# Attention probabilities turned by 32x32 blocks on VectorE and through DRAM instead of by TensorE transposes

## Chip, cores and metric

The kernel runs on one core of one Trainium2 chip. The metric is the device time of one execution in microseconds, as the median of several runs.

## What is computed

Two rows x of 1024 tokens by 512, float32. Cut to what matters:

```python
xn = layernorm(x)
q = rmsnorm(xn @ Wq.T, q_w)      # 32 heads of 128
k = rmsnorm(xn @ Wk.T, k_w)      # 8 kv heads of 128, 4 query heads on each
v = xn @ Wv.T
scores = q @ k.T / sqrt(128) + slope[head] * (j - i), masked to j <= i
s = softmax(scores) @ v          # heads side by side: 4096
s = s @ Wo.T                     # 4096 -> 512
g = silu(down(silu(xn @ w_gate.T) * (xn @ w_up.T)))   # inner size 1376
out = x + s * g
```

## The kernel before

Every matmul operand is held as two float32r parts, a high half (a ScalarE copy) and a low half (the value less its high half, made by VectorE or GpSimd), and every product is three matmuls: high x high, high x low, low x high.

For each of the 2 rows the kernel runs 8 units, one per kv group, and then the feed-forward part in chunks. A unit has 8 steps, one per query tile of 128 tokens. In step i, TensorE projects tile i+2 (`project`, lines 337 to 353), multiplies the attention tile of i-2 with w_o (`out_project`, 406), makes tile i's scores (`scores`, 366) in chunks of at most 512 keys per head, two score banks in turn, and between them turns and weighs tile i-1 block by block: `turn_probs` (381) turns the 128 keys of a block for the four heads by four TensorE transposes (line 388) into one of three ring banks, and `weigh` (392) multiplies the turned block with v (line 401). A unit has 36 such blocks. Then it turns q and k of tile i+1 (lines 359 and 364) in the same ring. The order is written out by hand in a `step` function for each engine, and each engine runs its own in order; semaphores count the results.

ScalarE squares the projections (line 569), stages v (574), copies the turned blocks' high halves out of the ring (`high_probs`, 597), takes exps in place with the row sum (`exp`, 589) and the high half of the attention tile (602). VectorE sums the squares (749), scales q and k (784), makes their low halves (790, 796), adds bias and mask and finds the row minimum (`bias`, 810, a main instruction and a read of the accumulator), divides the probabilities by their row sum (`divide`, 828), makes the blocks' low halves from the ring bank (`low_probs`, 818) and that of the attention tile (832), and adds to y (841). GpSimd has the chain of 13 small instructions for the norms (1016 to 1033), the low halves of w_qkv (1046), w_o (1052), v (1039, 1041) and of the feed-forward weights (1065, 1070). SyncE issues all transfers (`alone` is a wait, line 222). Probabilities lie in two buffers, one for even tiles and one for odd.

Of the kernel before, what the change touches and what calls it, by code (L numbers as in the profile page):

```python
# [47 lines left out]
CHUNK_WIDTH = [(i + 1) * P // HEAD_CHUNKS[i] for i in range(TILES)]  # L48
# [3 lines left out]
BEFORE = [TILES] + list(range(1, TILES))  # L52
RING_PER_STEP = 2
TURN_AT = [sum(BEFORE[1:i + 1]) - BEFORE[i] for i in range(TILES)] + [TURNS - TILES]
RBANKS = 3
RING = TURNS + RING_PER_STEP * TILES
RING_AT = [RING_PER_STEP - TILES]
for _i in range(TILES):
    RING_AT.append(RING_AT[-1] + BEFORE[_i] + RING_PER_STEP)
RING_AT[TILES] -= RING_PER_STEP  # L60

SKIPS = [RING_AT[2], RING_AT[5]]
RING_BANK = [(r + sum(r >= skip for skip in SKIPS)) % RBANKS for r in range(RING)]
assert (RING + len(SKIPS)) % RBANKS == 0
SLOTS = 4
LAG = 2

def ring_bank(r):

    return RING_BANK[r % RING]

def last_use(r):

    return next(q for q in range(r - 1, r - 2 * RBANKS, -1) if ring_bank(q) == ring_bank(r))

def turn_qk_at(i, turns, last):

    return turns - 1 if last and i >= TILES - 3 else turns + 1

def shape_of_step(i, first):

    chunks = G * HEAD_CHUNKS[i] if i < TILES else 0
    turns = 0 if first and i == 0 else TILES if i == TILES else BEFORE[i]
    return chunks, turns, max(chunks, turns + LAG if turns else 0)

def build(nc, x, w_qkv, w_o, w_ffn, q_norm, k_norm, rel, slopes, inv_slopes, ident_in, out):
    ctx = ExitStack()
    with ctx:
# [18 lines left out]
        probs = [sb("probs0", [P, G, S - P]), sb("probs1", [P, G, S])]  # L112
        pT_hi, pT_lo = sb("pT_hi", [P, SLOTS, G * P], F32R), sb("pT_lo", [P, SLOTS, G * P], F32R)
        attT_hi, attT_lo = sb("attT_hi", [P, G * P], F32R), sb("attT_lo", [P, G * P], F32R)
        natural = sb("natural", [P, 3 * NQK])
        qk = [natural[:, k * NQK:(k + 1) * NQK] for k in range(2)]
        qk_sq = natural[:, 2 * NQK:3 * NQK]
        v_nat = sb("v_nat", [P, VBUFS, P])
        rel_sb, ident = sb("rel_sb", [P, S]), sb("ident", [P, P])
# [3 lines left out]
        row_sum, rec = sb("row_sum", [P, 2, G]), sb("rec", [P, G])  # L123
        sq_sum, rq = sb("sq_sum", [P, G + 1]), sb("rq", [P, G + 1])
# [11 lines left out]
        probs0 = probs[0][:, :, :].rearrange("p g n -> p (g n)")  # L136
# [68 lines left out]
        def score_of(n, width, first):  # L205

            if first and n < G:
                return out_ps[:, 0:width] if n % 2 == 0 else ring_ps[:, ring_bank(1), 0:width]
            return score_ps[:, n % 2, 0:width]

        def early(t):

# [957 lines left out]
```

## Time and profile before

| | before |
|---|---|
| median of 3 runs | 2454.9 us (2453.91 to 2457.38) |
| the profiled execution's own time | 2455.46 us |
| its span | 2453.7 us, granted TensorE clock 0.998 |
| TensorE / VectorE / ScalarE / GpSimd busy | 99% / 69% / 50% / 31% |
| data moved | 92.19 MB, 38 GB/s on average |

The busy share is the time in which an engine had an instruction under way. The span runs from the first to the last instruction. A VectorE or ScalarE instruction may begin shortly before the one ahead has ended, so the sum of durations is somewhat above the busy time.

### The profile page before, as it was taken

Reading aid. Unit: us, or ns where it says so; the run is one execution under the profiler, and the core shown is the slowest. Engines: PE = TensorE matmul, PEld = TensorE weight load, DVE = VectorE, ACT = ScalarE, POOL = GpSimd, SP = SyncE. Lnnn points to the kernel's source line nnn. Section 1 sums busy time; section 2 is a strip of 40 time slices with the busy share of each in tenths; the row PEclk is TensorE's granted clock in tenths of the full one; section 3 lists DMA queues with packets and bytes.
Section 4 is the critical chain, followed back from the end, with each engine's and each line's share of the span. In section 5 each row is a group of like instructions: output and inputs, shape, how many; then the busy total and the mean of one; then the engine's idle time right before and its main releaser. Section 6 shows DMA issues by size and latency. Waiting matters only on the chain.

```text
span 2453.7 us, 37432 instructions
## 1 busy us (share of the span) xinstructions
PE 2422.6 (99%) x13232; PEld 2070.7 (84%) x13232; DVE 1693.7 (69%) x3788; ACT 1236.1 (50%) x2548; POOL 756.9 (31%) x2053
## 2 busy tenths in 40 slices
PE   7999999999999999999999999999999999999998
PEld 6888888888888888878888888888888888888887
DVE  7777777777778787823377787777777777777132
ACT  4555554555545555543355555555555545545333
POOL 2323231413233323244522232323232314131443
PEclk9999999999999999999999999999999999999999
DMA  3010000000000000023320101010000000010232
GB/s 130 1 40 4 27 18 27 18 27 18 27 18 27 18 27 18 27 91 125 112 78 1 44 1 44 1 44 1 27 18 26 18 27 18 1 44 14 90 103 103
DMA packets 23289, 92.19 MB, mean 38 GB/s; under 512 B 6592, under 2 KB 6720, under 8 KB 19136
## 3 DMA queue, kind: packets, MB, share of 16 engines
q1 hardware_dynamic: 23104, 89.80, 10.5%
q8 instruction: 106, 1.74, 0.3%
q14 instruction: 79, 0.65, 0.1%
HBM read 85.60 MB, written 4.19 MB: 37 GB/s over the span
## 4 chain that ended last, share of the span: by engine, by line
PE 96%; DVE 2%; ACT 1%; issue 1%; POOL 0%; DMA 0%; DVEq 0%; ACTq 0%; POOLq 0%
PE out_ps L401 17%; PE score_ps L377 16%; PE out_ps L414 14%; PE qkv_ps L351 14%; PE ring_ps L388 10%; PE qkv_ps L352 7%; PE score_ps L504 5%; PE qkv_ps L504 4%; PE ring_ps L520 4%; PE ring_ps L359 2%; PE out_ps L520 1%; PE ring_ps L364 1%; PE score_ps L351 0%; DVE y L997 0%; DVE xT_lo L868 0%
## 5 line engine op out<-in xcount | busy, mean ns | idle before, releaser
L597 ACT ACTIVATE pT_hi<-ring_ps 128x512 fp32r<-128x512 f32 x576 | 344.0, 599 | 509.8 <-PE ring_ps L388 497.2
L818 DVE TENSOR_TENSOR pT_lo<-ring_ps,pT_hi 128x512 fp32r<-128x512 f32 x576 | 396.8, 690 | 90.6 <-ACT pT_hi L597 86.0
L589 ACT ACTIVATE probs<-probs,low_min 128x896 f32<-128x896 f32 (+7 forms) x512 | 395.2, 774 | 50.4 <-DVE low_min L810 50.1
L1016 POOL TENSOR_SCALAR rs_x<-sq_sum 128x5 f32<-128x5 f32 x122 | 24.8, 203 | 1128.1 <-DVE sq_sum L749 1128.1
L388 PE MATMUL ring_ps<-ident,probs 128*128 128x128 f32 x2304 | 345.6, 273 | 0.0
L388 PEld LDWEIGHTS ring_ps<-ident,probs 128*128 128x128 f32 x2304 | 281.7, 140 | 42.1
L810 DVE CUSTOM_DVE_ANT_0 probs<-score_ps,rel_sb,slope 128x512 f32<-128x512 f32 (+5 forms) x504 | 301.7, 599 | 5.7 <-PE score_ps L377 4.3
L377 PE MATMUL score_ps<-kv_hi,qT_hi 128*128 128x320 f32 (+4 forms) x760 | 275.6, 363 | 3.0 <-DVE xT_lo L868 2.0
L401 PE MATMUL out_ps<-pT_hi,kv_hi 128*128 128x512 f32 x576 | 265.8, 461 | 2.9 <-DVE pT_lo L818 2.6
L377 PE MATMUL score_ps<-kv_hi,qT_lo 128*128 128x320 f32 (+4 forms) x760 | 261.0, 343 | 0.0
L377 PE MATMUL score_ps<-kv_lo,qT_hi 128*128 128x320 f32 (+4 forms) x760 | 260.3, 342 | 0.0
L828 DVE TENSOR_SCALAR probs<-probs,rec 128x896 f32<-128x896 f32 (+7 forms) x512 | 233.1, 520 | 4.5
L569 ACT ACTIVATE natural<-qkv_ps 128x640 f32<-128x640 f32 x124 | 87.7, 708 | 286.4 <-PE qkv_ps L352 286.4
L401 PE MATMUL out_ps<-pT_hi,kv_lo 128*128 128x512 f32 x576 | 227.5, 395 | 0.0
L401 PE MATMUL out_ps<-pT_lo,kv_hi 128*128 128x512 f32 x576 | 225.6, 392 | 0.0
L414 PE MATMUL out_ps<-o_hi,attT_hi 128*128 128x512 f32 x512 | 204.1, 399 | 0.0
L351 PE MATMUL qkv_ps<-qkv_hi,xT_hi 128*128 128x512 f32 x496 | 199.1, 401 | 1.8 <-DVE natural L784 1.8
L414 PE MATMUL out_ps<-o_hi,attT_lo 128*128 128x512 f32 x512 | 200.9, 392 | 0.0
L414 PE MATMUL out_ps<-o_lo,attT_hi 128*128 128x512 f32 x512 | 200.2, 391 | 0.0
L351 PE MATMUL qkv_ps<-qkv_hi,xT_lo 128*128 128x512 f32 x496 | 196.0, 395 | 0.0
L351 PE MATMUL qkv_ps<-qkv_lo,xT_hi 128*128 128x512 f32 x496 | 195.8, 395 | 0.0
L810 DVE CUSTOM_DVE_ANT_0 probs<-score_ps,rel_sb,low_min 128x320 f32<-128x320 f32 (+3 forms) x256 | 180.8, 706 | 21.0 <-PE score_ps L377 18.8
(178 smaller groups left out, 5293.5 us busy)
## 6 DMA issues: line engine op xcount, KB each, us to landing
qkv_raw<-w_ffn_dram SPq DMA_DIRECT2D x44, 768.0 KB, 4.2
qkv_raw<-w_qkv_dram SPq DMA_DIRECT2D x15, 1536.0 KB, 6.9
o_raw<-w_o_dram SPq DMA_DIRECT2D x16, 1024.0 KB, 4.8
o_raw<-x_dram SPq DMA_DIRECT2D x4, 1024.0 KB, 6.7
out_dram<-y SPq DMA_DIRECT2D x16, 256.0 KB, 3.7
probs<-x_dram SPq DMA_DIRECT2D x3, 1024.0 KB, 7.9
qkv_raw<-w_qkv_dram SPq DMA_DIRECT2D x4, 384.0 KB, 6.6
probs<-x_dram SPq DMA_DIRECT2D x2, 512.0 KB, 4.8
```

Of the source, the lines that this page charges most:

```text
L351: pe.matmul(acc[:, 0:BANK], a, w[:, c, 0:D], start=go, stop=end)
L352: mm = pe.matmul(acc[:, BANK:BANK + KV], a, w[:, c, D:NW], start=go, stop=end)
L377: mm = pe.matmul(score_of(n, hi - lo, first), q[:, i % 2, h * P:(h + 1) * P], kt[:, lo:hi], start=(q is qT_hi and kt is kT_hi), stop=(q is ...
L388: tr = pe.transpose(ring_ps[:, ring_bank(r), h * P:(h + 1) * P], probs[p % 2][:, h, j * P:(j + 1) * P], ident[:, :])
L401: mm = pe.matmul(out_ps[:, :], v[:, j * P:(j + 1) * P], pt[:, slot, :], start=(j == 0 and v is v_hi and pt is pT_hi), stop=(j == turns - 1 ...
L414: mm = pe.matmul(out_ps[:, :], a[:, h * P:(h + 1) * P], w[:, h * D:(h + 1) * D], start=(h == 0 and a is attT_hi and w is o_hi), stop=(h == ...
L504: mm = pe.matmul(acc, w[slot][:, at:at + P], xT[:, d, half * BANK:(half + 1) * BANK], start=(d == 0 and w is gu_hi and xT is xT_hi), stop= ...
L589: act.activation(row, row, ACT.Exp, scale=-1.0, bias=low_min[:, i % 2, h, HEAD_CHUNKS[i] - 1:HEAD_CHUNKS[i]], accum_out=row_sum[:, i % 2, ...
L597: act.activation(pT_hi[:, n % SLOTS, :], ring_ps[:, ring_bank(r), :], ACT.Copy).then_inc(ring_high, 1)
L810: dve.tensor_tensor_reduce(out=probs[i % 2][:, h, lo:hi], in0=score_of(n, hi - lo, first), in1=rel_sb[:, at:at + hi - lo], scale=slope[:, ...
L818: dve.tensor_tensor(out=pT_lo[:, n % SLOTS, :], in0=ring_ps[:, ring_bank(r), :], in1=pT_hi[:, n % SLOTS, :].bitcast(F32), op=ALU.subtract) ...
L828: dve.tensor_scalar(row, row, rec[:, h:h + 1], None, ALU.mult).then_inc(divided, 1)
```

## The change

TensorE no longer turns probabilities. After `exp`, VectorE turns each 32x32 square of a head's probabilities in place (`turn_blocks`); SyncE writes the tile to a DRAM tensor (`turned_out`) and reads it back with the four bands of 32 partitions exchanged, so that the tile lies turned in `pT`. To make the squares of a band contiguous, probabilities, `rel` and k are laid out by squares, and a score chunk is always up to 512 keys (before, the two chunks of a long tile had equal widths). The probabilities are not divided: `reciprocals` go through DRAM too (`rec_out_at`) and come back broadcast, and VectorE scales the attention tile (`scale_att`). A tile is weighed two steps after its scores (before one). ScalarE copies the high halves from `pT`; of the 36 low halves of a unit VectorE makes 23 and GpSimd 13 (`POOL_LOWS`), now from two SBUF operands. GpSimd also makes the attention tile's low half. The sum of squares is taken by ScalarE's accumulator, one square per head, and VectorE's reduce is dropped. The probabilities have one buffer instead of two; the freed ring banks give a third score bank and a second projection pair, in which q and k are turned in place. The out-projection lies three tiles behind.

Sizes:

```diff
+GROUP = 4
+BLOCKS, SQUARE = 4, 32
+HIGH_SLOTS, LOW_SLOTS = 4, 3
+SBANKS = 3
+POOL_LOWS = {3: (1,), 4: (0, 2, 4), 5: (1, 3, 5), 6: (1, 3, 5), 7: (1, 3, 5)}
```

SyncE:

```diff
+            def turn_probs(U, i):
+                t = tile(U, i)
+                slot = t % 2
+                alone(probs_turned, t * G)
+                if t > 2:
+                    back = (U - (i < 2)) * GROUPS + GROUP_AT[(i - 2) % TILES + 1]
+                    for k in range(2):
+                        alone(probs_back[k], (back + 1 - k) // 2 * BLOCKS * 16)
+                sp.dma_start(turned_out[slot, :, 0:(i + 1) * G * P], probs[:, 0:(i + 1) * G * P]).then_inc(probs_out, 16)
+                alone(rec_done, t)
...
+                sp.dma_start(rec_out_at[slot].rearrange("g p -> p g"), rec[:, i % 2, :], allow_slow_non_contiguous=True).then_inc(rec_out, 16)
+            def probs_home(U, i):
...
+                alone(probs_out, t * 16)
+                for part in range(GROUPS_IN[i]):
+                    lo, hi = keys_of(i, part)
+                    group = U * GROUPS + GROUP_AT[i] + part
+                    if group >= 2:
+                        done = chunks_to_group(group - 2)
+                        alone(low_by_dve, done // TURNS * DVE_LOW_AT[TURNS] + DVE_LOW_AT[done % TURNS])
+                        alone(low_by_pool, done // TURNS * POOL_LOW_AT[TURNS] + POOL_LOW_AT[done % TURNS])
+                    there = turned_out[slot].rearrange("(a r) n -> r a n", a=BLOCKS)
+                    run = (hi - lo) * G * SQUARE
+                    for k in range(BLOCKS):
+                        at = lo * G * P + k * run
+                        sp.dma_start(pT[k * SQUARE:(k + 1) * SQUARE, group % 2, 0:BLOCKS * run]
+                                     .rearrange("r (a n) -> r a n", a=BLOCKS), there[:, :, at:at + run]).then_inc(probs_back[group % 2], 16)
```

TensorE, a step:

```diff
             def step(U, i, first, last):
+                if not (last and i >= TILES - 2):
+                    project(U + (i + 2) // TILES, (i + 2) % TILES, first and i + 2 < TILES)
+                if not (last and i >= TILES - 1):
+                    turn_qk(U + (i + 1) // TILES, (i + 1) % TILES, first and i + 1 < TILES)
...
+                if not (first and i <= LAG):
                     out_project(U, i)
+                for k in range(sooner, chunks):
+                    scores(U, i, k, first)
...
+                    V, p = U - (i < LAG), (i - LAG) % TILES
+                    for j in range(p + 1):
+                        weigh(V, p, j, None if first and i == LAG else U * TILES + i - LAG)
```

ScalarE, the squares and then a step:

```diff
+                for h in range(G + 1):
+                    ins = act.activation(qk[i % 2][:, h * P:(h + 1) * P], acc[:, h * P:(h + 1) * P], ACT.Square,
+                                         accum_out=sq_sum[:, i % 2, h:h + 1])
...
+                    if not (first and i <= LAG):
                         high_att(U, i)
+                    for j in highs[:HIGH_SLOTS]:
+                        high_probs(V, p, j)
+                    highs = highs[HIGH_SLOTS:]
...
+                        high_q(N, n, first and n)
...
+                        squares(U + (i + 2) // TILES, (i + 2) % TILES, first and i + 2 < TILES)
...
+                        for h in range(G - 1):
+                            exp(U, i, h)
+                        for j in highs[:1]:
+                            high_probs(V, p, j)
+                        highs = highs[1:]
+                        exp(U, i, G - 1)
```

VectorE, a step and the wait that a tile's first bias has now:

```diff
+                    if not (first and i <= LAG):
+                        scale_att(U, i)
...
+                        scale_qk(N, n, first and n)
+                    for j in lows:
+                        if j < LOW_SLOTS:
+                            low_probs(V, p, j)
+                    lows = [j for j in lows if j >= LOW_SLOTS]
...
+                        low_q(N, n, first and n)
...
                         add_y(U, i, first)
+                    for k in range(sooner, chunks):
+                        bias(U, i, k)
+                        h, part = divmod(k, HEAD_CHUNKS[i])
+                        if part == HEAD_CHUNKS[i] - 1 and h >= 2:
+                            turn_blocks(U, i, h - 2)
...
+                        for h in (G - 2, G - 1):
+                            for j in lows[:1]:
+                                low_probs(V, p, j)
+                            lows = lows[1:]
+                            turn_blocks(U, i, h)
+                        reciprocals(U, i)
+                    for j in lows:
+                        low_probs(V, p, j)
...
+                if k == 0 and tile(U, i) > 1:
+                    dve.wait_ge(probs_out, (tile(U, i) - 1) * 16)
```

GpSimd, a step:

```diff
+                    if not (first and i <= LAG):
+                        low_att(U, i)
+                    for j in lows:
+                        if j < LOW_SLOTS:
+                            low_probs(V, p, j)
...
                         norms(U, i + 2)
...
+                    if i == LAG:
+                        low_o(U, 0)
+                        low_o(U, 1)
+                    for j in lows:
+                        if j >= LOW_SLOTS:
+                            low_probs(V, p, j)
+                    if 0 < i < TILES + 1:
+                        split_v(U, i - 1, first)
```

## Rows read from the trace of the kernel before

**Rows 1.** The page, part 1: busy us, share of the span, instructions.

```profile
PE 2422.6 (99%) x13232; PEld 2070.7 (84%) x13232; DVE 1693.7 (69%) x3788; ACT 1236.1 (50%) x2548; POOL 756.9 (31%) x2053
```

**Rows 2.** The page, part 4: the chain that ended last, shares by line.

```profile
PE out_ps L401 17%; PE score_ps L377 16%; PE out_ps L414 14%; PE qkv_ps L351 14%; PE ring_ps L388 10%; PE qkv_ps L352 7%; PE score_ps L504 5%; PE qkv_ps L504 4%; PE ring_ps L520 4%; PE ring_ps L359 2%; PE out_ps L520 1%; PE ring_ps L364 1%; PE score_ps L351 0%; DVE y L997 0%; DVE xT_lo L868 0%
```

**Rows 3.** A stretch of one unit: busy time of each engine, clock, DMA.

```profile
424.00:551.60 127.60, 127.58 (x725) 110.06 (x725) 96.77 (x221) 68.18 (x146) 37.92 (x126) 1.00 0.06 22
```

**Rows 4.** The chain in order of time (start us, us, what); then two timeline rows.

```profile
427.15 0.36 PE score_ps L377 x3
...
566.85 0.52 PE score_ps L377 x3
...
572.04 0.23 PE qkv_ps L351
...
576.20 2.75 PE out_ps L414 x12
578.95 0.69 PE score_ps L377 x3
579.63 0.44 PE ring_ps L388 x4
...
582.34 0.69 PE out_ps L401 x3
...
592.66 0.43 PE score_ps L377 x3
...
538.75 0.27 PE L377 MATMUL score_ps<-kv_lo,qT_hi 128*128 128x128 f32 x1
...
538.86 0.28 PE L377 MATMUL score_ps<-kv_hi,qT_lo 128*128 128x128 f32 x1
```

**Rows 5.** Groups by line and shape, VectorE: busy us, mean ns, idle before.

```profile
L810 DVE CUSTOM_DVE_ANT_0 probs<-score_ps,rel_sb,slope 128x512 f32<-128x512 f32 x128 | 95.5, 746 | 1.3
...
L828 DVE TENSOR_SCALAR probs<-probs,rec 128x1024 f32<-128x1024 f32 x64 | 43.9, 750 | 0.6
...
L810 DVE CUSTOM_DVE_ANT_0 probs<-score_ps,rel_sb,slope 128x128 f32<-128x128 f32 x56 | 19.2, 343 | 0.0
```

**Rows 6.** Timeline of VectorE in a step of tile 7: start us, us.

```profile
519.56 0.80 DVE L810 CUSTOM_DVE_ANT_0 probs<-score_ps,rel_sb,low_min 128x512 f32<-128x512 f32 x1
...
520.28 0.69 DVE L818 TENSOR_TENSOR pT_lo<-ring_ps,pT_hi 128x512 fp32r<-128x512 f32 x1
520.88 0.74 DVE L810 CUSTOM_DVE_ANT_0 probs<-score_ps,rel_sb,slope 128x512 f32<-128x512 f32 x1
```

**Rows 7.** Groups by line and shape, ScalarE.

```profile
L597 ACT ACTIVATE pT_hi<-ring_ps 128x512 fp32r<-128x512 f32 x576 | 344.0, 599 | 509.8 <-PE ring_ps L388 497.2
...
L589 ACT ACTIVATION_READ_ACCUMULATOR probs<-probs,low_min 128x1 f32 x512 | 99.4, 194 | 0.0
...
L589 ACT ACTIVATE probs<-probs,low_min 128x1024 f32<-128x1024 f32 x64 | 73.3, 1145 | 0.0
```

**Rows 8.** Groups by line and shape, GpSimd.

```profile
L1070 POOL TENSOR_TENSOR qT_lo<-qkv_raw,qT_hi 128x512 fp32r<-128x512 f32 x44 | 57.0, 1296 | 174.8 <-ACT qT_hi L643 174.8
```

**Rows 9.** Timeline of GpSimd: first instruction of a norm chain, and the one behind it.

```profile
427.44 0.20 POOL L1016 TENSOR_SCALAR rs_x<-sq_sum 128x5 f32<-128x5 f32 x1 [5.01 <-DVE sq_sum L749]
...
430.93 4.79 POOL L1052 TENSOR_TENSOR o_lo<-o_raw,o_hi 128x1024 fp32r<-128x1024 f32 x2
```

**Rows 10.** The page, part 6: DMA issues, KB each, median us to landing.

```profile
qkv_raw<-w_qkv_dram SPq DMA_DIRECT2D x15, 1536.0 KB, 6.9
o_raw<-w_o_dram SPq DMA_DIRECT2D x16, 1024.0 KB, 4.8
o_raw<-x_dram SPq DMA_DIRECT2D x4, 1024.0 KB, 6.7
```

**Rows 11.** Timeline at the end of the feed-forward part, GpSimd and VectorE.

```profile
1149.32 2.40 POOL L1065 TENSOR_TENSOR kv_lo<-qkv_raw,kv_hi 128x1024 fp32r<-128x1024 f32 x1
...
1149.46 2.81 DVE L997 TENSOR_TENSOR y<-y,probs 128x512 f32<-128x512 f32 x1 [2.11 <-ACT probs L737]
```

More of the change, by code:

```diff
@@ L441, in step @@
-                if first and i == 1:
-                    pe.wait_ge(qk_done, tile(U, 2))
-                    pe.wait_ge(v_staged, tile(U, 2))
-                elif not (last and i >= TILES - 2):
-                    project(U + (i + 2) // TILES, (i + 2) % TILES, qkv_ps, False)
-                late = last and TILES - 2 <= i <= TILES
-                spread = i == 1 and not first
-                if spread:
-                    out_project(U, i, range(0, 2))
-                elif not (first and i < 2) and not late:
-                    out_project(U, i)
@@ new lines, in step @@
+                    if first and i == 0 and U == 0:
+                        for t in range(HT, HT + 2):
+                            high_x(0, t)
+                    for j in highs:
+                        high_probs(V, p, j)
+                    if last and i == TILES - 2:
+                        high_gate_up(0, 0)
+                    if i == TILES:
+                        high_gate_up(1, 1)
+                        high_down(0, 0)
+                    if i == TILES + 1:
+                        high_down(1, 1)
@@ new lines, in step @@
+                    lows = [j for j in lows if j >= LOW_SLOTS]
+                    if first and i == 0:
+                        early_norms(tile(U, 2))
+                    if first and i == 1 and U == 0:
+                        for t in range(HT + 2, TILES):
+                            low_x(0, t)
+                    if not (last and i >= TILES - 1):
+                        low_q(N, n, first and n)
+                        if n:
+                            low_k(N, n, first)
+                    chunks = G * HEAD_CHUNKS[i] if i < TILES else 0
@@ new lines, in step @@
+                    if i == TILES - 1 and not last:
+                        low_k(U + 1, 0, False)
+                    if first and i == 0 and U == 0:
+                        for t in range(HT, HT + 2):
+                            low_x(0, t)
+                    if i < TILES:
+                        for h in (G - 2, G - 1):
[4 more added lines that the diff above has]
+                        reciprocals(U, i)
@@ L970, in unit @@
-                    for i in range(TILES + 2 if last else TILES):
+                            dve.wait_ge(rel_in, 16)
+                    for i in range(TILES + LAG + 1 if last else TILES):
                         step(U, i, first, last)
@@ L1147 @@
     slope = np.array([start * start ** i for i in range(H)], np.float32).reshape(HKV, 1, G)
+    order = (P, TILES, BLOCKS, SQUARE)
+    rel, seen = [np.broadcast_to(a, (P, S)).reshape(order).transpose(0, 2, 1, 3) for a in (u - p, u <= p)]
+    diagonals = [np.where(seen, rel + P * (n - 1), -MASK)[:, :, TILES - n:] for n in range(1, GROUP + 1)]
     arrays = {
```

696 lines of the change are left out of this document (323 added, 373 removed).

## Prediction

> **What bounds the kernel now.** First the page's busy line [rows 1]: TensorE is busy 2422.6 of 2453.7 us, VectorE 1693.7, ScalarE 1236.1, GpSimd 756.9. Then the chain of work that ended last [rows 2]: nearly all of it is TensorE, and 10% of it is line 388, the four transposes that turn each 128x512 block of probabilities. Then one kv group (8 query tiles) as a stretch [rows 3]: TensorE is busy for 127.58 of 127.60 us, VectorE for 96.77. So TensorE is the bound, and each block turned costs it the pitch of its four transposes, 0.44 us [rows 4]. The profiled execution took 2455.5 us, 0.02% above the median of 2454.9; its span is 2453.7. I sum against 2455.
>
> **What TensorE gains.** A group has 36 blocks: 36 x 0.44 = 15.8 us of 127.6. In 16 groups this is 253 us; the chain says 10%, 245 us. Score chunks are cut anew: tile 4 had two of 320 columns (0.43 us for three matmuls), now one of 512 (0.69) and one of 128, whose matmuls start 0.11 us apart, 0.33 [rows 4]. That is +0.16 for each of 4 heads, +0.6 per group. Tiles 5 and 6 add up to the same columns. TensorE's demand becomes 127.6 - 15.8 + 0.6 = 112.4 us per group. With nothing late that is 15.2 x 16 = 243 us off. The rest of the work is laid against it.
>
> **VectorE, per group.** Off: the divide, 750 ns at 128x1024 [rows 5], 4 per tile; the reduce of the squares; 13 of 36 low halves. On: block transposes of the same width as the divide. No row shows one. Below it can't be the divide's 750 ns; above I take two cycles for each element of the bias row, whose slope is (746 - 343)/384 = 1.05 ns per element [rows 5], so 2.2 us. The nearest row is the bias itself, one element per cycle: 0.1 + 0.133n us of pitch for n key tiles, 1.17 at n = 8, 22.4 us per group. The Trainium skill (VectorE: DVE Perf Modes, The three transpose paths) gives 311 ns for 128x128 in bf16; as an estimate that is the same price, and the sum would stay. Consecutive VectorE instructions overlap a little: a bias starts 0.6 after a low half, and a low half 0.72 after a second-part bias [rows 6]. With these pitches VectorE has about 92 us in 112: enough in total. It is the order that costs.
>
> **The order inside a step.** I call step i the one in which tile i's scores are made and tile i-2 is weighed, and count from the end of the weighing before. TensorE does: project (4.16), transpose q and k (0.55), out-projection (2.75), all scores, all weighing (0.69 a block) [rows 4]. So its demand in steps 0 to 7 is 13.7, 14.5, 10.3, 11.7, 13.7, 14.5, 15.9 and 17.4 us (0.7 of the 112.4 is spread over them). VectorE does y's addition after the out-projection and only then the biases, so they begin at 7.46 + 0.7 = 8.2 us into a step however early VectorE is free. Behind them stand, in order, four transposes, a reciprocal, and the late low halves. Before, low halves ran between the biases. The tail from 8.2 on is four biases and four transposes, a late low half and the reciprocal: at step 7, 4 x 1.52 (0.68 + 0.84 with the wait between the parts) + 4.7 + 0.6 + 0.2 = 11.6; step 6 10.5; step 5 9.5; step 4 7.8.
> What is late then:
> - Step 5: block 3's low half comes after all biases and two transposes: 8.2 + 5.0 + 1.8 + 0.6 = 15.6, its weighing ends at 16.4, and 0.5 is passed on from VectorE, which ends step 4 2.3 late: 2.4 over.
> - Step 6: likewise 16.5, then two weighings to 17.9, and 0.3 passed on: 2.3 over.
> - Step 7: block 4's low half at 17.3; block 5 waits for the fourth exp (1145 + 194 ns), its copy (0.6) [rows 7] and GpSimd's subtract, 1.3 us [rows 8]: ends 19.5. With 0.5 for the landing (below) 2.6 over.
> - Steps 0 and 1: GpSimd's norm chain waits for the squares, which ScalarE now makes as five instructions of about 0.4 and ends at 7.6; the chain is 3.5 long [rows 9]; GpSimd's blocks 3 and 5 are ready at 12.4 and 13.7. Step 0 weighs block 5 from 13.9 and 6 behind it, to 15.3: 1.6 over. In step 1 the landing (below) moves this by 0.5, and three blocks follow from 14.3, to 16.4: 1.9 over.
> - Step 2: 0.2. Step 3: GpSimd has the norm chain to 11.1 in step 2, then two low halves of w_o, 4.79 [rows 9], then v's: 16.7 against a step of 10.4. The subtract of the attention tile, now on GpSimd, stands behind it and releases the out-projection at 7.6 instead of 4.7: 2.8 over. Step 4: nothing.
> Sum: 1.6 + 1.9 + 0.2 + 2.8 + 2.4 + 2.3 + 2.6 = 13.8. A group takes 112.4 + 13.8 = 126.2 us, 1.4 less than now; 16 groups give -22.
>
> **The trip.** A tile's probabilities are one buffer now, so tile i+1's first bias waits for tile i's transfer out. Rows: 1 MB lands in 4.8 us with 8 KB rows, 1.5 MB in 6.9 [rows 10]; so 2 MB in 9.0. It starts at the end of the transposes, 0.4 to 2.3 into the next step; the first bias is at 8.2. After tile 7 that is 9.4: step 0's fourth score chunk waits for it, which hides behind the 12.4 above (three score banks run ahead); in steps 5 and 6 it is up to 0.4, in the amounts passed on. Home comes a half tile at a time: four transfers of 32 partitions with runs of 2 KB. Bounds for 1 MB: 4.8 (w_o's row) and 6.7 (x, rows of 2 KB) [rows 10]. I take 5.75, between, because each shares one trait with it: x the runs of 2 KB, w_o that it stands alone in its queue. A half can't start before the low halves of the half two before it are made; for tile 5 that is at 16.5 in step 6, so it lands 4.3 into step 7. ScalarE stands in order behind it: q's copy, the squares and the exps; VectorE's low_q too. Biases start at 8.75 instead of 8.2, the 0.5 above. The many 4-byte writes of the reciprocals ride behind the transfer out and cost nothing while that covers them; bare, up to 2 us. SyncE waits there too, with inv_slope, slope and w_o loads behind it; all are needed a step or more later, so nothing.
>
> **ScalarE**: squares 2.0 instead of 0.7 per tile, other moves equal; about 85 of 126 us. No cost but the one named. The FFN's matmuls don't change.
>
> **Ends of a row**, twice: the last tile's weighing waits for a trip of 9 + 5.75 us and the copies, against two short steps with a gate/up part each (10.4 + 5.6): 1.5; and the pipeline is a tile deeper, so the first three steps have little for TensorE beside VectorE's tails: 3.5. Together 5 each, 10.
>
> **Sum**: 2455 - 22 + 10 = 2443 us.
>
> **Rivals.**
> A. *Most of the gain arrives.* If the late low halves are earlier than laid out (transposes nearer 0.75, landing at 4.8), step 3's 2.8 and 2.2 of the rest stay: 112.4 + 5 = 117.4, 10.2 x 16 = -163, +10: 2302. For it: VectorE's 92 of 112. Against: the 8.2 is fixed by the program order.
> B. *The trip home binds; slower.* In place of 5.75 a half takes 6.7 or more, and the transfer out, a write, 1.5 longer than a read. Then step 7 starts its biases 1.5 late, step 1 its own 1, and steps 5, 6 and 0 wait 1 to 1.5 for the buffer: +6 per group, 132: 4.6 x 16 + 10 = +84: 2540. It decides from a landing of about 6.3, where a group is back at 127.6. For it: the 2 KB row has 6.7. The Trainium skill (SBUF - State Buffer, Door 1: The DMA port swizzle) says that a transfer that touches only 32 partitions reaches half of the ports, 189 GB/s at 1 MiB against 328; by that rule the half takes 5.5 us before its fixed part, and B is the case. No row here shows a 32-partition transfer.
> C. *VectorE and GpSimd hold each other; slower.* VectorE's low halves read two SBUF operands now (PSUM before). At 1149.46 a product of two SBUF tiles on VectorE took 2.81 us, where a block's low half takes 0.69: it ended 0.55 after GpSimd's instruction of 2.40 us that had begun 0.14 before it [rows 11]. If each late low half (8 on the path) is held for half of 1.3 us: +5, 131: 2530. 
> D. *Block transposes take two cycles an element*: +19 per group on tails that are bound in half of the steps, about +12: 2640.
> That the change doesn't do what it says, I can exclude: line 388 is gone.
>
> **Chances.** Forecast 0.36 (own range 2400 to 2485), A 0.24, B 0.20, C 0.14, D 0.06. 0.2% is 5 us, about what a measurement of this kernel tells from no change. In the forecast's case I give faster 0.22, same 0.06, slower 0.08. All of A is faster; of B and C, which stand on gains that may be larger than laid out, 0.02 is same and 0.02 faster. Faster 0.48, same 0.08, slower 0.44. The range takes in A to near 2330 and B and C to 2560; D and the far end of A are left out.
>
> **What would show it.** Right: line 388 gone; TensorE's idle named before out_ps weighing (by VectorE and GpSimd low halves) in steps 5, 6, 7, 0, 1, and before the out-projection by GpSimd once a group; biases starting 8.2 into a step; a transpose of 128x1024 near 1.2 us. A group near 126 us. Wrong: idle on ScalarE before pT_hi released by a DMA for long (B); low halves well above 0.7 us (C); transposes above 2 us (D); TensorE at 95% and more (A).

## The result and the profile after

The changed kernel takes 3322.9 us (median of 4 runs, 3301.8 to 3336.6) against 2454.4 of the kernel before: 1.3528 times as long, interval 1.3445 to 1.361. It is slower by 868 us where 12 us of gain were forecast, and outside the range. The profiled execution took 3313.2 us, 858 more than that of the kernel before (2455.5); the four runs lie up to 35 us apart. What an experiment takes off is counted from 3313.2. The page, part 1 with the granted clock of part 2, answers to [rows 1]; then part 4, the chain by engine, to [rows 2]:

```profile
PE 2458.1 (74%) x10928; PEld 2000.4 (60%) x10928; DVE 1687.3 (51%) x3452; ACT 1341.9 (41%) x3700; POOL 1223.1 (37%) x2389
...
PEclk8888897888888888889998888989888888888899
```

```profile
DMA 53%; PE 25%; DVE 8%; issue 5%; SPq 5%; POOL 2%; ACT 1%; DVEq 0%; POOLq 0%; ACTq 0%
```

TensorE has 2304 matmuls fewer and is yet busy for longer (2458.1 us against 2422.6), at a mean clock of 0.865. The chain is now more DMA than anything else; by line it is the transfer out (35%), the transfer home (8%) and the load of the slopes (7%). Part 6 of the page, the issues with KB each and the median us to landing, answers to [rows 10]:

```profile
pT<-turned_out SPq DMA_DIRECT2D x384, 256.0 KB, 7.3
...
turned_out<-probs SPq DMA_DIRECT2D x16, 2048.0 KB, 14.9
turned_out<-probs SPq DMA_DIRECT2D x16, 1792.0 KB, 16.0
...
turned_out<-probs SPq DMA_DIRECT2D x16, 1280.0 KB, 15.1
...
turned_out<-probs SPq DMA_DIRECT2D x16, 1024.0 KB, 8.6
...
turned_out<-probs SPq DMA_DIRECT2D x16, 256.0 KB, 11.3
...
slope<-slopes_dram SPq DMA_DIRECT2D x16, 2.0 KB, 16.0
```

A transfer out takes 8.6 to 16.0 us, and not in the order of its size: 256 KB take 11.3. One of 1792 KB (tile 6's) in the timelines of SyncE and VectorE at step 7 of a group in mid-row:

```profile
691.55 3.65 SPq L305 DMA_DIRECT2D pT<-turned_out  x8
695.38 0.34 SPq L315 DMA_DIRECT2D att<-rec_out_at  x1
695.98 0.34 SPq L283 DMA_DIRECT2D turned_out<-probs  x1
696.50 0.37 SPq L287 DMA_DIRECT2D rec_out_at<-rec  x1
```

```profile
702.45 0.67 DVE L878 TENSOR_TENSOR y<-out_ps,y 128x512 f32<-128x512 f32 x1
712.16 0.75 DVE L836 CUSTOM_DVE_ANT_0 probs<-score_ps,rel_sb,slope 128x512 f32<-128x512 f32 x1 [9.03 <-DMA turned_out<-probs]
```

The transfer is issued at 695.98 and the 512 writes of 4 bytes half a microsecond behind it. VectorE adds to y at 702.45, where the forecast has the first bias next, and stands still for 9.03 us until the landing at 712.14. The trace's packets show what the transfer does in that time: its own last packet ends at 705.42, the last of the 512 small ones at 705.6, and then nothing moves (columns as in [rows 3]; the last two are the busy share of the DMA engines and GB/s):

```profile
696.50:705.70 9.20, 7.71 (x40) 6.24 (x38) 3.26 (x4) 4.13 (x16) 3.35 (x12) 1.00 1.00 304
705.70:712.10 6.40, 0.00 (x0) 0.00 (x0) 0.00 (x0) 0.00 (x0) 0.45 (x3) 0.56 0.00 0
```

So for 6.5 of its 16.2 us the transfer has no packet under way, and only its landing is outstanding. Behind the bias wait the transposes, behind them the next transfer: one loop through one buffer, 128 times. The groups by waits (us in all, times, longest) and two rows of the chain:

```profile
PE score_ps L438 <- DVE low_min L836: 576.2, 79, 14.5
...
DVE probs L836 <- DMA turned_out<-probs: 481.2, 86, 12.0
```

```profile
712.97 1.65 PE score_ps L438 x3
714.62 1.28 PE third_ps L438 x3
```

The last rows show a second price of idling. The first three score matmuls behind the wait take 1.65 us, the next three 1.28, where three of that size take 0.69 in [rows 4]. The stretches before and behind 712 us:

```profile
702.50:712.00 9.50, 1.71 (x8) 1.09 (x6) 0.63 (x2) 0.48 (x4) 2.50 (x13) 0.71 0.27 101
712.00:718.00 6.00, 5.03 (x14) 4.00 (x15) 4.67 (x13) 2.48 (x4) 0.00 (x0) 0.61 0.00 0
```

TensorE is busy for 1.7 of 9.5 us, and in the 6 us behind them its granted clock is 0.61: the lower of its two levels (1.2 GHz) holds for most of the stretch. This is how TensorE comes to be busy for longer with fewer matmuls.

The steps can be measured one by one. The table gives the time from the turn of q and k of one tile to that of the next on TensorE's timeline (the first of the four transposes), mean over the 12 to 14 groups of both rows that touch no row end; the gap is the time from the last turn of the first row to the first of the second. The first line is the prediction's own layout (TensorE's demand plus the overrun it lists). The other kernels are those of the experiments.

| step | 7 | 0 | 1 | 2 | 3 | 4 | 5 | 6 | group | gap between rows |
|---|---|---|---|---|---|---|---|---|---|---|
| predicted | 20.0 | 15.3 | 16.4 | 10.5 | 14.5 | 13.7 | 16.9 | 18.2 | 126.2 | |
| before | | | | | | | | | 127.6 | 231 |
| after | 32.5 | 27.0 | 23.8 | 11.1 | 17.1 | 17.4 | 25.3 | 25.2 | 179.4 | 288 |
| g1_rec_turned | 24.9 | 19.9 | 22.0 | 10.4 | 15.7 | 14.5 | 17.0 | 20.3 | 144.7 | 275 |
| g4_all_three | 23.2 | 17.4 | 16.6 | 10.4 | 15.8 | 14.5 | 17.0 | 19.9 | 134.8 | 279 |
| h2_low_att_dve | 24.3 | 16.9 | 16.7 | 10.4 | 12.4 | 14.2 | 16.8 | 18.9 | 130.6 | 278 |
| i1_interleaved | 23.1 | 15.7 | 18.0 | 10.4 | 12.7 | 15.5 | 17.5 | 18.0 | 130.7 | 273 |
| k1_chunks_before_home | 23.8 | 14.7 | 16.3 | 10.4 | 12.6 | 15.5 | 17.5 | 19.9 | 130.6 | 263 |

A group takes 53 us more than forecast. By the same marks the 858 us against the kernel before divide so: 373 and 365 between the first and the last turn of each row, 56 in the gap, 59 behind the last turn of the second row, 4 ahead of the first. So about 115 us were lost at the two row ends, where the forecast had 10, and the rest of the miss inside the rows.

### The profile page after: what moved, and what is told of

Same layout as the page of the kernel before. It is cut to its first block, busy times and chain, and to the rows that moved or that the text cites. A ratio compares the mean times of both kernels' runs of the same rounds, so it can differ in the third digit from the quotient of the medians.

```text
span 3311.4 us, 37064 instructions
## 1 busy us (share of the span) xinstructions
PE 2458.1 (74%) x10928; PEld 2000.4 (60%) x10928; DVE 1687.3 (51%) x3452; ACT 1341.9 (41%) x3700; POOL 1223.1 (37%) x2389
## 2 busy tenths in 40 slices
DMA packets 238346, 428.44 MB, mean 129 GB/s; under 512 B 90560, under 2 KB 139840, under 8 KB 223936
## 4 chain that ended last, share of the span: by engine, by line
DMA 53%; PE 25%; DVE 8%; issue 5%; SPq 5%; POOL 2%; ACT 1%; DVEq 0%; POOLq 0%; ACTq 0%
DMA turned_out<-probs 35%; DMA pT<-turned_out 8%; DMA slope<-slopes_dram 7%; PE score_ps L438 5%; SPq L305 4%; PE out_ps L456 4%; PE score_ps L529 3%; PE qkv_ps L529 3%; DVE probs L836 3%; DMA rec_out_at<-rec 3%; DVE probs L847 2%; PE third_ps L438 2%; PE even_ps L545 2%; POOL pT_lo L1130 2%; PE out_ps L468 1%
## 5 line engine op out<-in xcount | busy, mean ns | idle before, releaser
L438 PE MATMUL score_ps<-kv_hi,qT_hi 128*128 128x512 f32 (+3 forms) x512 | 223.5, 437 | 579.4 <-DVE low_min L836 576.2
L1130 POOL TENSOR_TENSOR pT_lo<-pT,pT_hi 128x512 fp32r<-128x512 f32 x208 | 283.5, 1366 | 760.6 <-PE out_ps L456 493.9
L861 DVE TENSOR_TENSOR pT_lo<-pT,pT_hi 128x512 fp32r<-128x512 f32 x368 | 351.6, 968 | 412.8 <-ACT pT_hi L628 335.3
L836 DVE CUSTOM_DVE_ANT_0 probs<-score_ps,rel_sb,slope 128x512 f32<-128x512 f32 (+3 forms) x352 | 221.3, 639 | 536.5 <-DMA turned_out<-probs 371.6
L628 ACT ACTIVATE pT_hi<-pT 128x512 fp32r<-128x512 f32 x576 | 330.7, 622 | 275.7 <-DMA pT<-turned_out 201.4
L847 DVE STREAM_TRANSPOSE probs<-probs 128x896 f32<-128x896 f32 (+7 forms) x512 | 378.6, 761 | 2.9 <-ACT probs L619 2.4
L1122 POOL TENSOR_TENSOR attT_lo<-att,attT_hi 128x512 fp32r<-128x512 f32 x128 | 167.6, 1310 | 490.9 <-ACT attT_hi L633 490.9
L456 PEld LDWEIGHTS out_ps<-pT_hi,kv_hi 128*128 128x128 f32 x576 | 129.3, 224 | 162.3 <-DVE pT_lo L861 84.8
L438 PE MATMUL score_ps<-kv_lo,qT_hi 128*128 128x512 f32 (+3 forms) x512 | 210.3, 411 | 0.0
L438 PE MATMUL score_ps<-kv_hi,qT_lo 128*128 128x512 f32 (+3 forms) x512 | 207.8, 406 | 0.0
## 6 DMA issues: line engine op xcount, KB each, us to landing
turned_out<-probs SPq DMA_DIRECT2D x16, 1536.0 KB, 11.3
```

The costliest lines, as they stand in the source:

```text
L438: mm = pe.matmul(score_all[n % SBANKS][:, 0:(hi - lo) * P].rearrange("p (b j r) -> p b j r", b=BLOCKS, r=SQUARE), q[:, i % 2, h * P:(h + 1 ...
L456: mm = pe.matmul(out_ps[:, :], v[:, j * P:(j + 1) * P], pt[:, slot, :], start=(j == 0 and v is v_hi and pt is pT_hi), stop=(j == i and v i ...
L628: act.activation(by_block(pT_hi[:, n % HIGH_SLOTS, :]), landed(i, j), ACT.Copy).then_inc(probs_high, 1)
L836: dve.tensor_tensor_reduce(out=by_head[:, h, lo * BLOCKS:hi * BLOCKS, :], in0=score_all[n % SBANKS][:, 0:n_keys * P].rearrange("p (m r) -> ...
L847: dve.transpose(row, row).then_inc(probs_turned, 1)
L861: dve.tensor_tensor(out=by_block(pT_lo[:, n % LOW_SLOTS, :]), in0=landed(i, j), in1=by_block(pT_hi[:, n % HIGH_SLOTS, :].bitcast(F32)), op ...
```

## Experiments

Each was run once beside the kernel before (k1 twice), whose runs here lie between 2453 and 2457 us. The two runs of k1 lie 4 us apart and the four of the changed kernel 35, so a difference of a few us between single runs tells nothing.

### What makes the landing late

**e1_rec_rows** writes the same 2 KB of reciprocals as 128 rows of 16 bytes, not as 512 single values (in another order, so the attention tile is scaled by other rows' values).

```diff
-sp.dma_start(rec_out_at[slot].rearrange("g p -> p g"), rec[:, i % 2, :], allow_slow_non_contiguous=True)
+sp.dma_start(rec_out_at[slot].rearrange("g p -> (g p)").rearrange("(p g) -> p g", g=G), rec[:, i % 2, :])
```

> The reciprocals are written to DRAM as 128 rows of 16 bytes instead of 512 elements of 4 bytes (they come back in another order, so the attention rows are scaled by the wrong factors; nothing else changes). The profile of the changed kernel has VectorE's first bias of a tile waiting for the transfer out of the tile before in 86 of 128 cases, and in the chain that transfer has 35%: a large one is 14.9 to 16.0 us from issue to landing where 9.0 was forecast. Theory 1: the 512 small writes, issued right behind it on the same 16 engines, delay its landing. Then the transfers out land about 5 us sooner, and 128 tiles x 4 to 5 us take the time from 3320 to 2700 to 2850. Theory 2: its landing is set by what stands ahead of it in the queue and by its own bytes. Then the time stays within 3%, 3220 to 3400.

Measured 2810.2 us: 503 us off, by one access pattern, as theory 1 has it. Its issues (part 6 of the page):

```profile
turned_out<-probs SPq DMA_DIRECT2D x16, 2048.0 KB, 11.0
turned_out<-probs SPq DMA_DIRECT2D x16, 1792.0 KB, 10.6
...
turned_out<-probs SPq DMA_DIRECT2D x16, 1280.0 KB, 5.2
...
turned_out<-probs SPq DMA_DIRECT2D x16, 1024.0 KB, 3.9
...
rec_out_at<-rec SPq DMA_DIRECT2D x128, 2.0 KB, 5.5
```

1792 KB land in 10.6 us instead of 16.0 and 1280 KB in 5.2 instead of 15.1, though nothing of these transfers was changed. In the 1280 KB transfer a part of this is a chain: its packets start 0.8 us behind the issue instead of 4.5, since the transfers home ahead of it are through sooner.

**g1_rec_turned** brings each value to its own row: VectorE turns the reciprocals (0.21 us) and four transfers with 4 rows of 128 bytes each take them out.

> The reciprocals are turned by one block transpose of 32x32 squares on VectorE and then leave in 4 transfers of 4 partitions with 128 B in each (the after kernel: 512 writes of 4 bytes), so the kernel computes what the reference does. Theory 1 (the 512 small writes hold back the landing of the transfer out ahead of them): as with the reciprocals written as rows, 2810 us, within 2780 to 2880, and a 1024 KB transfer out lands in 4 to 5 us. Rival (it was the number of writes per partition, not their size, or the wrong values, that made the run with rows short): 3100 us or more.

Measured 2771.3 us, 542 off (9 us under the range of theory 1); 1280 KB land in 4.5 us. The page's packets under 512 B fall from 90560 to 27072, the 496 a tile that are gone. Two rows of its issues:

```profile
turned_out<-probs SPq DMA_DIRECT2D x16, 1792.0 KB, 9.7
...
turned_out<-probs SPq DMA_DIRECT2D x16, 256.0 KB, 10.6
```

The packets of the three traces show that it is the landing and not the data that was late. Medians over the 16 transfers of 1792 KB: the last packet ends 9.4 us behind the issue in the changed kernel, 9.2 in e1, 9.2 in g1; the landing comes 6.6, 1.2 and 0.5 us behind that. Over the 112 transfers of 512 KB and more this last stretch is 5.1 us in the median and 9.0 at most in the changed kernel, 1.0 and 2.2 in e1, 0.4 and 0.6 in g1. It varies: in 19 of the 112 it was 2 us or less with the same writes behind. The 256 KB transfer is not such a case: it takes 10.6 us in g1 too, and 5.3 in g2 below, where it no longer stands behind tile 7's transfers home and a load of w_qkv in their queue. Whether small writes from another queue would delay a landing as well was not tried.

**e2_out_constant** keeps the small writes, but sends constant data out, and no bias waits for the transfer (the probabilities stay out of what is weighed). **e3_home_quarter** brings only one of the four column bands home.

> The transfer out reads a constant tile of the same shape (the high half of x turned) from the third tile on, so that VectorE's biases need not wait for it to leave the one buffer of probabilities; it still starts when the transposes are made, and still must land before the trip home starts (the probabilities used are wrong). Theory 1: the loop of biases, transposes and transfer out, one tile after the other, is what sets the time. Then the 630 us that VectorE waits before biases for DMA go for the most part, and the time falls to 2500 to 2700, near what was laid out. Theory 2: the trip home is late as well and takes the place of that wait at once (ScalarE's copies wait for it in order). Then the time stays above 2950.

> The trip home moves only one of the four column bands (a quarter of the bytes and of the descriptors, as many transfers); the others stay zero, so the weights are wrong. Theory 1: the transfers home of a tile, issued just before the transfer out of the next, stand ahead of it in the 16 engines and hold it for 4 to 5 us. Then transfers out of large tiles land in about 11 us instead of 15, and the time falls by 128 x 3 to 4 us to 2800 to 2950. Theory 2: the engines are idle half of the time and the queue ahead does not matter. Then the time falls by less than 3%.

Measured 2950.8 and 3068.7 us; e2 lies on the bound of its theory 2, e3 between its two. Without the bias's wait 362 us go, less than by mending the writes: the transfer home stands behind the same late landing and takes the wait over (in the changed kernel ScalarE waited 201.4 us for it, in 76 times). The two rows are of e2:

```profile
DVE pT_lo L862 <- ACT pT_hi L629: 522.6, 189, 15.7
...
ACT pT_hi L629 <- DMA pT<-turned_out: 391.4, 101, 14.4
```

With three quarters of the data home left out (e3) 245 us go; the transfers out still take 12.6 to 13.0 us from 1280 KB up, so the home's load is a part of it, the small writes the larger one. The parts overlap and can't be added.

**e4_lows_on_dve** (POOL_LOWS empty: no low half on GpSimd).

> All 36 low halves of a kv group on VectorE, none on GpSimd. Theory 1 (the DMA loop sets the time, the low halves lie beside it): VectorE gets 208 more instructions of 0.7 us, of which those late in a step lengthen the loop; the mean of a low half falls from 968 ns to 720 to 800 ns since GpSimd reads less beside it; the time is within 3% of 3320. Theory 2 (VectorE and GpSimd holding each other sets the time): it falls below 3150.

Measured 3257.1 us. The low half falls from 968 to 765 ns, and only 56 us go, in one run, as theory 1 has it.

### What holds the mended kernel

**g2_out_on_act**: g1, the transfer out issued by ScalarE at the end of its step. **g3_loads_moved**: g1, both slope tables loaded once, the weights' loads behind the transfer home. **g4_all_three**: both.

> g1_rec_turned, and the transfer out is issued by ScalarE behind its last exp and copy of the step instead of by SyncE, where it stands behind a wait for the reciprocals' return and the loads. Theory 1 (the transfers still wait in one queue behind loads and one another): 2810 less 100 to 250 us; transfers out at steps 0, 1, 4 and 5 land in 5 to 8 us. Rival (what is left is the loop itself, bias, transposes, transfer, bias, with one buffer): less than 50 us off, or slower, since ScalarE waits there for VectorE's transposes with its copies behind.

> g1_rec_turned, and slope and inv_slope are loaded once ahead of everything (the after kernel: 128 rows of 16 B and 20 B once a unit, 16 and 11.7 us to landing), and the loads of w_qkv and w_o stand behind the transfer home of their step instead of ahead of the transfer out. Theory 1: the 14 waits for slope (12.7 us each in the after kernel, some 148 us in all, 7 to 10 us each once the writes are gone) go, and the transfers out behind w_qkv and w_o land 5 us sooner: 2810 less 120 to 250 us. Rival (the waits move on to the next transfer): less than 60 us off.

> All changes of the three before it. If each of them takes away its own wait: 2450 to 2600 us, TensorE's granted clock above 0.95. If the loop over one buffer binds (theory of the loop): 2650 us or more, with the wait for the transfer out still first among VectorE's.

Measured 2661.9, 2766.1 and 2644.3 us. The queue was worth 109, within what was expected; the loads only 5 (g3 against g1) and 18 (g4 against g2), the rival's case. g4 missed the 2450 to 2600 of its first theory and lies just under the loop's 2650. In g3 the slope's waits were gone, and the wait for the transfer out took their place: 157.6 us in 54 times (g1: 107.5 in 31). Under g2 that wait is down to 9.6 us.

**h1_lows_dve** (g4, all low halves on VectorE), **h2_low_att_dve** (g4, the attention tile's subtract on VectorE), **h3_no_bias_wait** (g4, the transfer out reads a constant and no bias waits), **h4_best** (h1, h2 and a feed-forward load a step earlier).

> g4_all_three with all 36 low halves of a kv group on VectorE, none on GpSimd. In g4_all_three a group takes some 133 us (before: 127.6) and the low halves 0.997 us on VectorE and 1.38 on GpSimd. Theory of contention (rival C of the prediction: the two hold each other): the low half falls to about 0.75 us, and although 13 more of them stand on VectorE the tails of steps 5, 6, 7, 0 and 1 get shorter: 30 to 100 us off, 2545 to 2615. Rival (VectorE's order and load bind, the change was right to give GpSimd 13): 13 x 0.7 us more in a group lie on the tails, +30 to +100 us, 2675 to 2745.

> g4_all_three with the subtract of the attention tile back on VectorE (the kernel before had it there; the changed kernel has it on GpSimd, 1347 ns against 0.7 us on VectorE). In g4_all_three TensorE waits 52 us for it before the out-projection, once a group for long. If the prediction's 2.8 us per group at step 3 is right: 45 us off for that, and the 0.65 us a tile that the subtract is shorter is mostly hidden behind the scores: 2570 to 2610. Rival (step 3 has another limit behind it, 14.5 us either way): less than 15 us off.

> g4_all_three, but the transfer out reads a constant region of the same size, so that the next tile's first bias waits for nothing; the trip and all its other waits stay (and a transfer out is issued only when the one before has landed). What is weighed is not the probabilities. It is what a second buffer of probabilities would give. In g4_all_three the waits of VectorE for the transfer out are 31 us in all. Theory (the loop over one buffer is no longer the bound once the small writes and the queue are mended): 10 to 40 us off, 2605 to 2635. Rival (the loop still sets the pace of steps 6 and 7): 60 us or more off.

> h1_lows_dve and h2_low_att_dve together, and the load of the feed-forward part's second chunk a step earlier, ahead of the transfers home of tile 6 (in g4_all_three the gap between the two rows is 279 us against 231 before, with waits of 10 and 13 us for these loads). If the three add up: 2450 to 2550 us. To beat the kernel before it would have to be under 2454. If VectorE becomes the bound (its busy time then some 1850 us): 2600 or more.

Measured 2649.7, 2574.0, 2604.6 and 2570.7 us. h1: neither expectation; the low half fell from 997 to 801 ns, and 13 more of them stand on VectorE: no gain. h2: 70 us off, as expected; step 3 falls from 15.8 to 12.4, where the prediction has a term of 2.8. h3: 40 off, so the loop over one buffer is no longer the main loss. h4: neither expectation, the parts do not add up; with h2 in, h1 and the load bring 3 us, not to be told from nothing.

**i1_interleaved** (h2 with another order) tests the prediction's main stall term, that the late low halves stand behind all biases:

```diff
-                for k in range(sooner, chunks):
+                ahead = min(SBANKS, chunks)
+                for k in range(sooner, ahead):
+                    scores(U, i, k, first)
+                for j in blocks[:LOW_SLOTS]:
+                    weigh(V, p, j, None if first and i == LAG else U * TILES + i - LAG)
+                for k in range(max(sooner, ahead), chunks):
...
+                for j in blocks[LOW_SLOTS:]:
+                    weigh(V, p, j, None if first and i == LAG else U * TILES + i - LAG)
...
+                            for j in lows[:1]:
+                                if j < 2 * LOW_SLOTS:
+                                    low_probs(V, p, j)
+                                    lows = lows[1:]
```

The first two parts are TensorE's, the last is VectorE's, behind the last bias of heads 2 and 3; ScalarE's copies move between the exps too.

> h2_low_att_dve, and the order inside a step changed: TensorE weighs blocks 0 to 2 after the first three score chunks instead of after all of them, ScalarE copies the high halves of blocks 4 and 5 between the exps, and VectorE makes up to two of the late low halves behind the biases of heads 2 and 3 instead of behind all biases. The prediction puts the overruns of steps 5, 6, 7, 0 and 1 (8.8 us a group of its 13.8) down to that order; in h2_low_att_dve these steps stand at 16.8, 18.9, 24.3, 16.9 and 16.7 us against TensorE's demand of 14.5, 15.9, 17.4, 13.7 and 14.5. Theory of the order: 5 to 9 us a group, 2574 less 80 to 140: 2430 to 2495; the half that goes home in step 6 leaves earlier too. Rival (the trip home and the loop over one buffer bind these steps whatever the order): less than 30 us off, 2545 or more.

**i2_chunk_early** is i1 with the second feed-forward load a step earlier, **i3_lows_dve** is i2 with all low halves on VectorE.

> i1_interleaved, and the second feed-forward chunk's load a step earlier. In h2_low_att_dve TensorE waits at each end of a row about 17 us for that chunk (its load stands behind eight transfers home); the gap between the rows is 278 us against 231 before. If that wait alone made the gap: 20 to 40 us off in two rows. If the next trip takes its place (h4_best had 276.5 for the gap): less than 5 us off.

> i2_chunk_early with all low halves on VectorE. With the late low halves between the biases VectorE has no free place for 13 more: 13 x 0.7 us less 23 x 0.3 us of contention is 2 us a group more: +0 to +40 us. Should contention be the larger term here, 10 to 40 us off.

Measured 2575.5, 2576.7 and 2562.1 us. i1 brings nothing: steps 6, 7 and 0 get 3.3 us shorter in all by the table, steps 1, 4 and 5 as much longer. The order moved time between steps, and the group as a whole is bound by something else. i2: nothing. i3: 15 off, the case in which contention is the larger term (the low half takes 695 ns in it, 703 in h4, with GpSimd free of these and of the attention tile's).

**k1_chunks_before_home**: i3, the first two feed-forward loads issued ahead of tile 5's transfers home. **k3_no_bias_wait**: k1 with the constant transfer out of h3.

> i3_lows_dve, and the loads of the feed-forward part's first two chunks are issued in step 5 of a row's last unit, ahead of that tile's transfers home, which wait for the low halves of step 6 (in i1_interleaved, GpSimd's low half of the first chunk starts 11.6 us after TensorE has nothing else, and the gap between the rows is 270 to 274 us against 231 before). If the loads queued behind that wait make the row ends: 15 to 25 us off at each, 30 to 50 in all: 2512 to 2532. If it is the last tiles' trips: less than 10 off.

> k1_chunks_before_home with the transfer out reading a constant region, so that no bias waits for it; what is weighed is not the probabilities. It bounds what a second buffer for them would give here. In g4_all_three it gave 40 us. If the loop over one buffer is what the reordering ran into (theory now): 60 us or more under k1_chunks_before_home. If the trip home alone binds: 40 or less.

Measured 2550.0 us (1.0393 of before, 1.0362 to 1.0423) and 2556.6. The loads in the queue were 12 us of the row ends, between the two expectations; 263 us of gap against 231 remain. k3 is not faster: in this version no wait of a bias for the transfer out is seen to cost anything. k1 is the best version found, 23% under the changed kernel and still 4% over the one before. Of the 97 us between the profiled executions 32 are in the gap, 32 behind the last turn of the second row, and 28 between the first and last turns of both rows: two thirds of what is left is at the row ends, which only the 12 us of the loads touched. VectorE's timeline at the end of step 6 in it shows what stands in the group:

```profile
657.13 0.71 DVE L841 CUSTOM_DVE_ANT_0 probs<-third_ps,rel_sb,slope 128x512 f32<-128x512 f32 x1
...
658.49 0.69 DVE L868 TENSOR_TENSOR pT_lo<-pT,pT_hi 128x512 fp32r<-128x512 f32 x1
659.09 3.09 DVE L852 STREAM_TRANSPOSE probs<-probs 128x896 f32<-128x896 f32 x3
...
662.41 0.65 DVE L881 TENSOR_TENSOR att<-out_ps,att 128x512 f32<-128x512 f32 x1
662.98 0.81 DVE L812 TENSOR_TENSOR natural<-even_ps,rq 128x640 f32<-128x640 f32 x1
```

VectorE passes from one step's transposes straight to the next step's work. In the stretch from one turn of q to the next around step 7 (first row below) it is busy for 18.73 of 23.38 us, TensorE for 20.36 at a clock of 0.85; from there to the next (second row) VectorE for 8.60 of 15.05:

```profile
534.70:558.08 23.38, 20.36 (x85) 15.85 (x84) 18.73 (x36) 11.14 (x29) 3.20 (x15) 0.85 0.63 189
558.08:573.13 15.05, 14.65 (x76) 11.69 (x75) 8.60 (x25) 6.87 (x27) 3.61 (x15) 1.00 0.69 204
```

## Why the prediction was wrong, point by point

- **The failed step** is the trip: "2 MB in 9.0. It starts at the end of the transposes ... the first bias is at 8.2", and "the many 4-byte writes of the reciprocals ride behind the transfer out and cost nothing while that covers them". The price came from loads alone in their queue [rows 10]; the writes were bounded by their own time only. What they did was to hold back the landing of the transfer ahead of them, by 5.1 us in the median behind its last packet (0.4 in g1), so that 1792 KB took 16.0 us and 1280 KB 15.1. Shown by e1 and g1: 503 and 542 of 858 us. Without them the price was fair: in g1 1280 KB land in 4.5 us and 1536 KB in 6.7 (6.9 for the load of [rows 10]); 2 MB take 10.5, not 9.0 (their first packet starts 3.6 us behind the issue, while a transfer home is still moving), and 256 KB 10.6, since they stand in the queue behind tile 7's transfers home and a load of w_qkv. The sum had no term for either.
- **The loop** was seen ("tile i+1's first bias waits for tile i's transfer out"), but only as up to 0.4 us in steps 5 and 6. With 4 to 11 us more (against g1) to every landing but that of 256 KB it carries them into nearly every step; the same late landing holds the transfer home, which is why e2 gets only 362 back.
- "SyncE waits there too, with inv_slope, slope and w_o loads behind it; ... so nothing": wrong. The slope's load took 16.0 us to land, and the first bias of 14 units waited for it (147.6 us in all in the profile after). But the queue as a whole, with the transfer out behind the others, counts for more: 109 us (g2), the loads 5 to 18.
- **Row ends**, "together 5 each": they grew by 56 and 59 us in the changed kernel and are still 32 each longer in k1. The feed-forward loads behind the transfers home were 12 in all. The rest, the last tiles' trips in a stretch with little other work, was not taken apart.
- **Clock**: the sum takes every matmul at the full clock. With the idle gaps the mean granted clock is 0.865, and the matmuls behind a gap take longer (1.28 us against 0.69 above). No term stood for it.
- **Right**: transposes of 128x1024 take 1230 ns, where 1.17 us were taken; rival D falls with it, and so does A, which wanted 0.75 and a landing at 4.8. Groups of after, VectorE and GpSimd, by line and shape:

```profile
L847 DVE STREAM_TRANSPOSE probs<-probs 128x1024 f32<-128x1024 f32 x64 | 77.5, 1230 | 0.0
...
L861 DVE TENSOR_TENSOR pT_lo<-pT,pT_hi 128x512 fp32r<-128x512 f32 x368 | 351.6, 968 | 412.8 <-ACT pT_hi L628 335.3 <-PE out_ps L456 77.2
L1130 POOL TENSOR_TENSOR pT_lo<-pT,pT_hi 128x512 fp32r<-128x512 f32 x208 | 283.5, 1366 | 760.6 <-PE out_ps L456 493.9 <-ACT pT_hi L628 266.5
```

- **Rival C** is there (968 ns where 0.69 stood in [rows 6]), but small in time: 56 us in e4, none in h1, 15 in i3. (Its sum comes to about 2525, not 2530.)
- **The layout of a step** held once the trip was mended: in g4 steps 1, 2 and 5 stand within 0.2 us of it, steps 3, 4, 6, 0 and 7 are 1.3, 0.8, 1.7, 2.1 and 3.2 above. Its reason is not borne out: if "it is the order that costs", i1 should have been 80 us faster or more, by what was expected of it. The subtract of the attention tile behind GpSimd's work was right (h2).
- **Rival B** fits the kernel once the writes are mended: 132 us a group, g4 has 134.8. Its price for a half tile was right as well, and the forecast's 5.75 us too low. The page's 4.9 us is for one of the four transfers of a half; from the first issue to the last landing a half of 1 MB takes 7.0 us in the median, in g1 as in g4, and ScalarE's copies wait 109.9 us for it in g4, in 44 times, which is B's own sign. In g4 the half that step 7 waits for was issued at 538.99 and let ScalarE start at 547.74, with tile 6's transfer out issued at 540.87, in between. But of B's steps only 7, 0 and 6 are late; 5 and 1 are not, and no run tested B by itself.
- **Why a half takes so long**: its runs of 2 KB alone do not explain it. The first row is g1 with only transfers home under way (32 partitions each), the second the kernel before with loads of x (128 partitions, rows of 2 KB). The DMA engines are busy throughout in both, and move 225 GB/s and 373:

```profile
573.00:576.00 3.00, 3.00 (x15) 2.58 (x15) 1.42 (x2) 0.63 (x1) 1.29 (x1) 0.82 1.05 225
```

```profile
1122.00:1125.00 3.00, 3.00 (x14) 2.44 (x13) 0.66 (x1) 1.58 (x2) 1.62 (x2) 1.00 1.03 373
```

The two differ in partitions and in where in DRAM they read; a transfer home with more partitions was not tried. The Trainium skill (SBUF - State Buffer, Door 1: The DMA port swizzle), from which the prediction takes 189 GB/s for 32 partitions, agrees in kind. But that figure is the page's measurement of a whole 1 MiB transfer. The 5.5 us worked out from it, an estimate, therefore have no fixed part to come, and by them B would not have been the case.

- **What stays open**: what ties steps 7 and 6 in k1, where VectorE, the trip and the clock all come near, and what the row ends are made of.

## To carry to other kernels

Price a transfer by its landing with what is issued behind it, not by its bytes: many small scattered writes to DRAM can hold back the landing of the large one ahead, and if a buffer's reuse hangs on that landing, the delay is paid every time round. Turn small values on chip and write them in long rows. When work is moved from the bound engine into a loop over one buffer, draw the loop and ask what one more microsecond in it costs before summing the rest; and take idle TensorE time at more than its length, since the granted clock fell with it here. And lay out the row ends as carefully as the steady part: in the best version they are two thirds of what is lost.

## What the runs showed of the hardware

- 512 writes of 4 bytes, issued 0.5 us behind a transfer of 1792 KB, moved its landing from 9.7 us to 16.0, while its last packet stayed at 9.2 to 9.4. The Trainium skill (DMA: Bandwidth & Descriptors, Queues, rings and completion order) says that the semaphore's increment lands only after every earlier write of that DMA engine. Here later writes of the same queue delayed it as well, which that rule doesn't say.
- A block transpose of 32x32 squares in float32 takes 1230 ns for 1024 columns, 1094 for 896, 962 for 768, 304 for 128: about 1.03 ns for each further column.
- Four transfers into 32 partitions each, with runs of 2 KB, moved 225 GB/s with the DMA engines busy; a load into 128 partitions with rows of 2 KB moved 373.
- A square of 128x128 with its sum on ScalarE is two instructions, 289 and 223 ns, the second only the read of the accumulator.
- Low halves from two SBUF tiles, mean on VectorE: 968 ns beside GpSimd doing the same, 765 and 801 with only the attention tile's left on GpSimd (e4, h1), 695 to 703 with neither there (h4, i3, k1).
